# Two engines take attention a's outputs out of PSUM: in whole tiles, or in halves of the columns

## The chip, the cores and the metric

The kernel runs on one core of a Trainium2 chip. Its engines are TensorE (PE in the profile; PEld is its loading of weights), VectorE (DVE), ScalarE (ACT), GpSimd (POOL) and SyncE (SP), which here only issues DMAs. Each engine works through its own instructions in order; across engines they meet only through semaphores. The metric is the device time of one execution in microseconds, from the median of several runs.

## The reference

Sixteen sequences of 512 tokens and 256 features go through four sublayers, each added to its input after a layer norm: attention a, a gated feed-forward network, attention b, and the same network again. Attention a, cut to what matters here:

```python
q, k, v = proj(Wq, bq), proj(Wk, bk), proj(Wv, bv)          # 16 heads of 16 features
scores = jnp.einsum('bhsd,bhtd->bhst', q, k) * SCALE
scores = jnp.where(mask, scores, -jnp.inf)                  # |i - j| <= 32, or i < 4, or j < 4
attn = jax.nn.softmax(scores, axis=-1)
out = jnp.einsum('bhst,bhtd->bhsd', attn, v)                # then out @ Wo.T + bo
```

## The kernel before

The sixteen sequences are pipelined. A table (`AT`) gives each step of a sequence a place, a sequence starts 425 places after the one before, and `STEPS` is the list of all steps sorted by place. Every engine walks through this one list and issues its own part, so the order on each engine is written out by hand; there is no planner at run time. Some 132 us of the trace are one such turn, and in it steps of three or four sequences stand between each other: while attention a of one sequence is in its outputs, attention b and the feed-forward networks of earlier ones run.

Scores, probabilities' denominators and outputs share a ring of five PSUM banks (`s_bank`, 128 partitions by 512 columns of float32). `ring_places` fixes which step takes which bank; before a step writes, `pair_free` on TensorE waits until the bank's last owner has been read out, for every bank that the step takes, and only then go its matmuls.

Attention a's output of one group of four heads is the step `AV` (`a_values`, lines 919, 926 and 933: matmuls on a 64-row half of the array each). It takes two banks: one for the upper and one for the lower half of the key rows. The two have to be added. This is done in two steps:

- `AH` on ScalarE (`a_take_half`, line 1178): copies the second bank, 128x512 float32, into the SBUF tile `o_raw` (two buffers in turn), and raises `a_half`;
- `AT` on VectorE (`take_out`, line 1359): waits for `a_half`, adds the first bank to `o_raw` in place, and raises `o_taken`.

`AO` on SyncE (`store_output`, line 633) waits for `o_taken` and writes `o_raw` to DRAM. The next step of TensorE that needs the two banks waits for `a_half` (second bank) and for `o_taken` (first bank); mostly it is a pair of attention b's numerator scores, `b_pair`, line 967, which ScalarE exponentiates at line 1155 (`probs_B`). There are four groups in a sequence, so 64 takes in all: in a turn they start, in this profile's order, at places 545, 602, 627 and 648 (called first to fourth take below). Attention b's outputs need one bank and one copy (line 1365) and are not touched.

Other lines that the steps below speak of: 946 and 1165 are attention b's denominator scores and their exponentials with a sum (each followed by a short read of the accumulator), 1148 are attention a's exponentials, 1183 and 1431 split transposed inputs, 1218 writes the rotated queries and keys, 1412 to 1422 are the layer norm's last steps on VectorE, 1496 and 1498 take attention values out in pieces of 256 columns, 574 and 711 are DMA issues of SyncE (packed queries and keys, the next input).

Of the kernel before, what the change touches and what calls it, by code (L numbers as in the profile page):

```python
# [8 lines left out]
ACT = mybir.ActivationFunctionType  # L9
AX = mybir.AxisListType  # L10

SEQS, S, D = 16, 512, 256
# [4 lines left out]
GROUPS = 4  # L17
# [289 lines left out]
def build(nc, x_in, Wq, bq, Wk, bk, Wv, bv, Wo, bo, Wqkv, Wout, bout, w_gate, w_up, w_down,  # L307
# [7 lines left out]
    with ctx:  # L315
        def sb(name, shape, dt):
            return ctx.enter_context(nc.sbuf_tensor(name, shape, dt))

        def sem(name):
            return ctx.enter_context(nc.semaphore(name))  # L320
# [68 lines left out]
        o_raw = [sb(f"o_raw{i}", [P, S], F32) for i in range(2)]  # L389
# [46 lines left out]
        a_half = sem("a_half")  # L436
# [11 lines left out]
        o_taken = sem("o_taken")  # L448
# [63 lines left out]
        def score_bank(kind, n, q, e=0):  # L512
            return s_bank[RINGS[kind, n, q][e][0]]
# [213 lines left out]
        def _(pe):  # L727
# [15 lines left out]
            for n, bank in enumerate(banks):  # L743
# [4 lines left out]
                if n >= len(all_banks):  # L748
                    last = n - len(all_banks)
                    pe.wait_ge(w_taken if last < NSPLIT else w_staged, last + 1 if last < NSPLIT else last - NSPLIT + 1)  # L750
                for c0, a in bank:
                    last = pe.transpose(all_banks[n % len(all_banks)][:, c0:c0 + P], a, eye[:, :])
# [10 lines left out]
            def pair_free(kind, n, q):  # L763

                for _, before in RINGS[kind, n, q]:
                    if before is None:
                        continue
                    kind, n, r, e = before
                    if kind == "A1":
                        pe.wait_ge(a1_taken, r * UNITS["A"] + 2 * n + e + 1)  # L770
                    elif kind == "TM":
                        pe.wait_ge(ntopT_ready, r + 1)
                    elif kind == "A2":
                        pe.wait_ge(a_exp, r * UNITS["A"] + 2 * n + e + 1)
                    elif kind == "AV" and e:
                        pe.wait_ge(a_half, r * GROUPS + n + 1)
                    elif kind == "AV":
                        pe.wait_ge(o_taken, TAKE["A", n, r] + 1)
                    elif kind == "DP":
                        pe.wait_ge(den_exp, r * UNITS["D"] + 2 * n + e + 1)  # L780
                    elif kind == "DT":
                        pe.wait_ge(rden_ready["B"], r + 1)
                    elif kind == "BV":
                        pe.wait_ge(o_taken, TAKE["B", n, r] + 1)
                    else:
                        pe.wait_ge(b_exp, r * UNITS["N"] + 2 * n + e + 1)
# [92 lines left out]
            def a_pair(kind, p, q):  # L879
                pair_free(kind, p, q)  # L880
                if p == 0 and kind == "A1":
                    pe.wait_ge(blocks_ready, q + 1)
                    a_far_first(q)
                elif p == 0:
                    pe.wait_ge(ntopT_ready, q + 1)
                    a_far_second(q)
                else:
                    if kind == "A1" and p == 1 and q == 0:
                        pe.wait_ge(c_in, 16 * NC)
                        pe.wait_ge(fills_in, 48)  # L890
                    if kind == "A1" and p % 2:
                        pe.wait_ge(a_packed[p // 2], (q + 1) * 96)
                    elif p == 1:
                        pe.wait_ge(ntop_in, (q + 1) * 128)
                    a_near(kind, p, q)

            def turn_maxima(q):
                pair_free("TM", 0, q)
                pe.wait_ge(ntop_ready, q + 1)
                bank = score_bank("TM", 0, q)[0:2 * HEADS, :]  # L900
                pe.matmul(bank[:, 0:GLOBALS], ntop[:, NT, :], glob_sel[:, :], start=True, stop=True, skip_group_check=True)
                for t in range(NT):
                    a = GLOBALS if t == 0 else 0
                    last = pe.matmul(bank[:, t * P + a:(t + 1) * P], ntop[:, t, :], eye_bf[:, a:], start=True, stop=True,
                                     skip_group_check=True)
                last.then_inc(ntop_turned, 1)

            def a_values(j, q):

                v = v_aug["A"]  # L910
                bank = [score_bank("AV", j, q, half) for half in range(2)]
                pair_free("AV", j, q)
                if j == 0:
                    pe.wait_ge(v_glob_in, (q + 1) * 16)
                    pe.wait_ge(gu_taken, gu_use("V", 1, "VA", q) + 1)
                pe.wait_ge(a_exp, q * UNITS["A"] + 2 + 4 * (j + 1))
                for t in range(NT):
                    for c in range(4):
                        pe.matmul(bank[t % 2][32 * c:32 * c + DH + 1, 0:GLOBALS], v[:, t, head(j, c), :],
                                  probs_gq[:, t, head(j, c), :], start=t < 2, stop=t >= 2,  # L920
                                  tile_position=(0, 32 * c), skip_group_check=True)

                for c in range(4):
                    for half, columns in enumerate((slice(S // 2, S), slice(GLOBALS, S // 2))):
                        r = slice(HB * half, HB * half + HB)
                        pe.matmul(bank[half][32 * c:32 * c + DH + 1, columns], v_glob[r, head(j, c), :], probs_gk[r, columns],
                                  start=False, stop=False, tile_position=(HB * half, 32 * c), skip_group_check=True)
                for t in range(NT):
                    for c in range(4):
                        for half in range(2):  # L930
                            r = slice(HB * half, HB * half + HB)
                            col, a, b = window(t, half)
                            last = pe.matmul(bank[half][32 * c:32 * c + DH + 1, a:b], v[r, t, head(j, c), :],
                                             probs["A"][r, (4 * j + c) % RING["A"], col:col + b - a], start=False, stop=True,
                                             tile_position=(HB * half, 32 * c), skip_group_check=True)
                last.then_inc(a_used, 1)
# [196 lines left out]
        def _(act):  # L1133
# [38 lines left out]
            def a_take_half(j, q):  # L1172

                take = TAKE["A", j, q]
                if take // 2:
                    act.wait_ge(o_out[take % 2], take // 2 * 16)
                act.wait_ge(a_used, q * GROUPS + j + 1)
                act.activation(o_raw[take % 2][:, :], score_bank("AV", j, q, 1)[:, :], ACT.Copy).then_inc(a_half, 1)

            def x_high(block, q):  # L1180
                for k in range(KT):
# [38 lines left out]
            for n in range(NSPLIT, NBANKS):  # L1220
                act.wait_ge(w_turned, n + 1)
                bank, m = all_banks[n % len(all_banks)], n - NSPLIT
                if m < 8:
                    dst, k, half = (st_gT, st_uT)[m // 4], m // 2 % 2, m % 2
# [5 lines left out]
            for _, kind, n, block, q in STEPS:  # L1230
                if kind == "A2E":
                    a_exponential(2 * n, q)
                    a_exponential(2 * n + 1, q)
                elif kind == "TC":
                    keep_maxima(q)
                elif kind == "AH":
                    a_take_half(n, q)
                elif kind == "DE":
                    den_exponential(2 * n, q)
                    den_exponential(2 * n + 1, q)  # L1240
                elif kind == "NE":
                    b_exponential(2 * n, q)
                    b_exponential(2 * n + 1, q)
                elif kind == "XH":
                    x_high(block, q)
                elif kind == "GT":
                    half_tanh(block, n, q)
                elif kind == "T1":
                    qk_step(block, n, q)
                elif kind == "W2":  # L1250
                    rot_high_step(n, q)
# [3 lines left out]
        def _(dve):  # L1255
# [29 lines left out]
            for t in range(KT):  # L1285
                for c2 in range(2):
# [3 lines left out]
                    last = dve.tensor_copy(dst, a)  # L1290
# [63 lines left out]
            def take_out(kind, j, q):  # L1354

                take = TAKE[kind, j, q]
                if kind == "A":
                    dve.wait_ge(a_half, q * GROUPS + j + 1)
                    dve.tensor_tensor(o_raw[take % 2][:, :], o_raw[take % 2][:, :], score_bank("AV", j, q)[:, :], ALU.add)\  # L1359
                        .then_inc(o_taken, 1)  # L1360
                    return
                if take // 2:
                    dve.wait_ge(o_out[take % 2], take // 2 * 16)
                dve.wait_ge(b_used, q * GROUPS + j + 1)
                dve.tensor_copy(o_raw[take % 2][:, :], score_bank("BV", j, q)[:, :]).then_inc(o_taken, 1)
# [317 lines left out]
```

## Time and profile before

| | us |
|---|---|
| median of 3 runs | 2285.48 (2284.11 to 2287.06) |
| the profiled execution's own time | 2279.23 |
| its span, first to last instruction | 2277.5 |
| TensorE busy | 1931.6 (85%) |
| ScalarE busy | 1445.5 (63%) |
| VectorE busy | 1387.9 (61%) |

The span is that of one execution under the profiler; 1.7 us of its own time lie around it. Busy times are those of the whole span, and each stretch of a turn has another limit, so the chain of work that ended last is what tells where a microsecond counts. The mean granted clock of TensorE is 0.936 of full speed.

### The profile page before, as it was taken

How to read it: one execution, taken by the hardware profiler on the slowest of the kernel's cores; microseconds unless marked ns; L12 is line 12 of the kernel's file. 1: busy time of each engine (PE TensorE's matmuls, PEld its weight loads, DVE VectorE, ACT ScalarE, POOL GpSimd, SP SyncE). 2: the span in 40 equal slices, each digit the busy share in tenths (PEclk: the TensorE clock that was granted, in tenths of full speed). 3: DMA queues.
4: the chain of work that ended last, by engine and by line, in shares of the span. 5: the costliest groups of instructions: out<-in, count | busy, mean ns of one | idle time of the engine just before them, and what ended most of it. 6: DMA issues, size and time to landing. Idle time of an engine off the chain costs nothing.

```text
span 2277.5 us, 63345 instructions
## 1 busy us (share of the span) xinstructions
PE 1931.6 (85%) x25221; PEld 1387.7 (61%) x25221; DVE 1387.9 (61%) x2971; ACT 1445.5 (63%) x3580; POOL 781.6 (34%) x1131
## 2 busy tenths in 40 slices
PE   5677879889898989989798998979898898989785
PEld 4463657666675756657576665757566675756444
DVE  5363657576575757657575765757576675755534
ACT  1227666676767667676766767676676767667580
POOL 0023233334323333332333343233334334334331
PEclk8798999999999999999999999999999999999887
DMA  7214344252434424243442524343342434333221
GB/s 186 71 42 95 60 114 92 76 111 72 105 67 121 85 78 109 69 105 68 118 88 78 108 71 106 66 122 84 82 106 74 110 73 109 83 90 85 70 63 34
DMA packets 129636, 201.87 MB, mean 89 GB/s; under 512 B 26768, under 2 KB 60560, under 8 KB 129312
## 3 DMA queue, kind: packets, MB, share of 16 engines
q1 hardware_dynamic: 129344, 197.80, 36.2%
q8 instruction: 205, 3.36, 0.6%
q14 instruction: 87, 0.71, 0.1%
HBM read 67.87 MB, written 51.52 MB: 52 GB/s over the span
## 4 chain that ended last, share of the span: by engine, by line
PE 57%; ACT 16%; DVE 11%; SPq 6%; DMA 5%; issue 4%; POOL 1%; POOLq 0%; ACTq 0%; DVEq 0%
PE gu_bank L1051 15%; PE d_bank L1067 7%; ACT s_bank L1165 6%; PE gu_bank L1079 6%; SPq L574 5%; PE s_bank L982 5%; PE s_bank L946 4%; ACT probs_B L1155 4%; PE gu_bank L1015 3%; PE gu_bank L1002 3%; PE s_bank L812 2%; PE s_bank L967 2%; DMA pack_b<-src_b 2%; PE gu_bank L1025 2%; PE s_bank L820 2%
## 5 line engine op out<-in xcount | busy, mean ns | idle before, releaser
L1165 ACT ACTIVATE s_bank<-s_bank 128x512 f32<-128x512 f32 x1024 | 602.5, 591 | 171.9 <-PE s_bank L946 171.3
L1574 POOL TENSOR_TENSOR h<-tmp,h 128x512 fp32r<-128x512 f32 x192 | 252.0, 1313 | 448.0 <-DVE h L1455 448.0
L1155 ACT ACTIVATE probs_B<-s_bank 128x512 f32<-128x512 f32 x640 | 334.5, 611 | 47.4 <-PE s_bank L967 44.8
L1051 PE MATMUL gu_bank<-xT,w_g 128*128 128x256 f32 x1536 | 231.5, 294 | 28.2 <-DVE tmp L1438 23.1
L946 PE MATMUL s_bank<-pack_b 48*128 48x512 f16 x1024 | 182.7, 400 | 82.4 <-DMA pack_b<-src_b 69.4
L1051 PE MATMUL gu_bank<-xT,w_u 128*128 128x256 f32 x1536 | 239.2, 296 | 3.2 <-DVE tmp L1444 0.5
L1051 PEld LDWEIGHTS gu_bank<-xT,w_g 128*128 128x128 f32 x1536 | 205.0, 196 | 55.2 <-DVE tmp L1438 37.6
L1194 ACT ACTIVATE tmp<-gu_bank 128x512 f32<-128x512 f32 x192 | 114.6, 597 | 192.7 <-PE gu_bank L1051 184.5
L1067 PE MATMUL d_bank<-w_d,h 128*128 128x256 f32 x1536 | 225.5, 289 | 3.3 <-POOL h L1574 3.3
L1051 PEld LDWEIGHTS gu_bank<-xT,w_u 128*128 128x128 f32 x1536 | 205.5, 196 | 36.6 <-issue 20.4
L1438 DVE SCALAR_TENSOR_TENSOR tmp<-tmp,gu_bank 128x512 f32<-128x512 f32 x192 | 130.8, 682 | 148.3 <-ACT tmp L1194 146.8
L1591 POOL TENSOR_SCALAR_AFFINE_SELECT probs_B<-probs_B 128x256 f32<-128x256 f32 x512 | 193.1, 412 | 42.7 <-ACT probs_B L1155 42.6
L1067 PEld LDWEIGHTS d_bank<-w_d,h 128*128 128x128 f32 x1536 | 196.8, 189 | 17.1 <-issue 7.9
L1165 ACT ACTIVATION_READ_ACCUMULATOR s_bank<-s_bank 128x1 f32 x1024 | 196.2, 192 | 0.0
L1444 DVE TENSOR_TENSOR tmp<-tmp,gu_bank 128x512 f32<-128x512 f32 x192 | 132.0, 688 | 83.9 <-PE gu_bank L1051 82.0
L1557 POOL TENSOR_TENSOR veps<-mv,eps 128x4 f32<-128x4 f32 x64 | 12.9, 202 | 489.6 <-DVE mv L1408 489.6
L967 PE MATMUL s_bank<-pack_b 48*128 48x512 f16 (+3 forms) x1024 | 116.7, 310 | 72.9 <-DVE o_raw L1359 32.4
L1328 DVE TENSOR_REDUCE top<-s_bank 128x4 f32<-128x512 f32 x256 | 161.0, 684 | 5.0 <-PE s_bank L820 5.0
L1148 ACT ACTIVATE probs_A<-s_bank 128x512 f32<-128x512 f32 x256 | 133.5, 602 | 46.2 <-PE s_bank L820 45.3
L982 PE MATMUL s_bank<-probs_B,v_aug_B 128*16 128x512 f32 (+3 forms) x2048 | 156.2, 447 | 2.6 <-POOL probs_B L1591 2.3
L812 PE MATMUL s_bank<-band,eye_bf 64*64 64x512 bf16 x1024 | 110.4, 419 | 27.7 <-DMA pack_a<-src_a 14.0
L946 PEld LDWEIGHTS s_bank<-pack_b 48*128 48x128 f16 x1024 | 41.4, 94 | 145.7 <-DMA pack_b<-src_b 72.1
(140 smaller groups left out, 3320.6 us busy)
## 6 DMA issues: line engine op xcount, KB each, us to landing
pack_b<-src_b SPq DMA_DIRECT2D x768, 64.0 KB, 2.5
pack_a<-src_a SPq DMA_DIRECT2D x384, 64.0 KB, 2.3
x<-in_L_attn_a_x_dram SPq DMA_DIRECT2D x32, 512.0 KB, 4.9
o_scr_A<-o_raw SPq DMA_DIRECT2D x64, 256.0 KB, 2.4
o_scr_B<-o_raw SPq DMA_DIRECT2D x64, 256.0 KB, 2.1
xn<-o_scr_A SPq DMA_DIRECT2D x32, 256.0 KB
rden_on<-r_scr_A SPq DMA_DIRECT2D x32, 256.0 KB
x_scr<-x SPq DMA_DIRECT2D x16, 512.0 KB, 2.9
```

The lines of the kernel that those rows point to most:

```text
L812: pe.matmul(bank[e][HB * half:HB * half + HB, :], eye_of(e), rows_of(band, e, half), start=True, stop=False, tile_position=(HB * e, HB * h ...
L946: pe.matmul(score_bank("DP", n, q, e)[:, :], pack_b[r, j % 2, 0, 0, tile, t * P:(t + 1) * P], pack_b[r, j % 2, 0, 1, tile, :], start=True, ...
L967: last = pe.matmul(bank[e][:, c0:c0 + S - t * P], pack_b[r, j % 2, 1, 1, tile, t * P:(t + 1) * P], pack_b[r, j % 2, 1, 0, tile, t * P:S], ...
L982: last = pe.matmul(bank[32 * c:32 * c + DH, t * P:S], v_aug["B"][:, t, head(j, c), 0:DH], probs["B"][:, n, c0:c0 + S - t * P], start=t == ...
L1051: last = pe.matmul(bank[:, f * D:(f + 1) * D], plain(w[:, k, c:c + P], exact), plain(given[:, k, half * D:(half + 1) * D], exact), start=k ...
L1067: last = pe.matmul(bank[:, t, :], plain(h[part][:, i % 2, c:c + P], exact), plain(w_d[:, 2 * pair + f, :], exact), start=pair == 0 and f = ...
L1079: last = pe.matmul(bank[:, :], w_part[:, k, n * P:(n + 1) * P], given[part][:, k, :], start=k == 0 and i == 0, stop=k == KT - 1 and i == 2)
L1155: act.activation(probs["B"][:, i, :], score_bank("NP", n // 2, q, n % 2)[:, :], ACT.Exp, scale=SM_SCALE)\
L1165: act.activation(bank[:, :], bank[:, :], ACT.Exp, scale=SM_SCALE, accum_out=den[:, 0, j, 2 * tile + e, t:t + 1]).then_inc(den_exp, 1)
L1328: dve.reduce_max(dst, a, AX.X).then_inc(a1_taken, 1)
L1574: pool.tensor_tensor(h[1][:, i % 2, :], tmp[:, i % 2, :], h[0][:, i % 2, :].bitcast(F32), ALU.subtract)\
L1591: ins = pool.affine_select(a, a, [[0, 2], [1, P]], ALU.is_ge, 0.0, base=0, channel_multiplier=-1)
```

## The change

ScalarE copies the second bank in two instructions of 256 columns each and raises `a_half` after each. VectorE adds in two instructions of 256 columns each, waiting for one more of `a_half` before each, and raises `o_taken` after the second only. TensorE's wait for the second bank counts two per take. The same elements are computed from the same operands; no step moves to another place in any engine's list.

```diff
                     elif kind == "AV" and e:
-                        pe.wait_ge(a_half, r * GROUPS + n + 1)
+                        pe.wait_ge(a_half, 2 * (r * GROUPS + n + 1))
...
                 act.wait_ge(a_used, q * GROUPS + j + 1)
-                act.activation(o_raw[take % 2][:, :], score_bank("AV", j, q, 1)[:, :], ACT.Copy).then_inc(a_half, 1)
+                for columns in (slice(0, S // 2), slice(S // 2, S)):
+                    act.activation(o_raw[take % 2][:, columns], score_bank("AV", j, q, 1)[:, columns], ACT.Copy).then_inc(a_half, 1)
...
                 if kind == "A":
-                    dve.wait_ge(a_half, q * GROUPS + j + 1)
-                    dve.tensor_tensor(o_raw[take % 2][:, :], o_raw[take % 2][:, :], score_bank("AV", j, q)[:, :], ALU.add)\
-                        .then_inc(o_taken, 1)
+                    for n, columns in enumerate((slice(0, S // 2), slice(S // 2, S))):
+                        half = o_raw[take % 2][:, columns]
+                        dve.wait_ge(a_half, 2 * (q * GROUPS + j) + n + 1)
+                        last = dve.tensor_tensor(half, half, score_bank("AV", j, q)[:, columns], ALU.add)
+                    last.then_inc(o_taken, 1)
                     return
```

## Rows read from the trace of the kernel before

**Rows 1.** The profile's page: the chain that ended last, shares by engine and line.
```profile
PE 57%; ACT 16%; DVE 11%; SPq 6%; DMA 5%; issue 4%; POOL 1%; POOLq 0%; ACTq 0%; DVEq 0%
```
**Rows 2.** The two lines of the take: instructions, idle before, who waits (us, times).
```profile
L1178 ACT ACTIVATE o_raw<-s_bank x64: 576/597/597, 78.6 to 2046.1; 128x512 f32<-128x512 f32 x64
...
L1359 DVE TENSOR_TENSOR o_raw<-o_raw,s_bank x64: 686/689/689, 79.2 to 2046.8; 128x512 f32<-128x512 f32 x64
  ACT o_raw L1178: 119.0, 63
...
  PE s_bank L967: 32.4, 27
  PE s_bank L946: 1.4, 1
```
**Rows 3.** The chain in order of time (start, length, what): a first take; first and last.
```profile
92.40 0.60 ACT o_raw L1178
...
1081.68 0.60 ACT o_raw L1178
1082.31 0.70 DVE o_raw L1359
1083.01 0.14 issue
1083.14 0.42 PE s_bank L967 x4
1083.57 1.89 ACT probs_B L1155 x4
...
2046.13 0.60 ACT o_raw L1178
```
**Rows 4.** Groups by shape, all of the span: busy, mean ns | idle before.
```profile
L1148 ACT ACTIVATE probs_gq<-s_bank 128x256 f32<-128x256 f32 x16 | 6.1, 384 | 4.2 <-PE s_bank L875 4.2
L1496 DVE TENSOR_TENSOR v_aug_A<-gu_bank,v_bias 128x256 f32<-128x256 f32 x64 | 23.9, 414 | 2.8 <-PE gu_bank L1002 2.7
```
**Rows 5.** ScalarE in order of time (start, length), around a first take.
```profile
1071.56 0.19 ACT L1165 ACTIVATION_READ_ACCUMULATOR s_bank<-s_bank 128x1 f32 x1
1071.65 0.59 ACT L1165 ACTIVATE s_bank<-s_bank 128x512 f32<-128x512 f32 x1
1081.68 0.60 ACT L1178 ACTIVATE o_raw<-s_bank 128x512 f32<-128x512 f32 x1 [0.59 <-PE s_bank L933]
1082.17 1.08 ACT L1155 ACTIVATE probs_B<-s_bank 128x512 f32<-128x512 f32 x2
1083.56 2.06 ACT L1155 ACTIVATE probs_B<-s_bank 128x512 f32<-128x512 f32 x4 [0.30 <-PE s_bank L967]
```
**Rows 6.** VectorE in order of time, the same stretch.
```profile
1082.31 0.69 DVE L1359 TENSOR_TENSOR o_raw<-o_raw,s_bank 128x512 f32<-128x512 f32 x1 [1.14 <-ACT o_raw L1178]
1082.91 0.15 DVE L1412 SCALAR_TENSOR_TENSOR newton<-root 128x4 f32<-128x4 f32 x1
1083.10 0.16 DVE L1415 TENSOR_TENSOR newton<-newton,veps 128x4 f32<-128x4 f32 x1
1083.50 1.38 DVE L1422 TENSOR_SCALAR xn<-x,mv,root 128x256 f32<-128x256 f32 x4
1086.14 1.29 DVE L1431 TENSOR_TENSOR xT<-gu_bank,xT 128x512 fp32r<-128x512 f32 x2 [0.40 <-ACT xT L1183]
```
**Rows 7.** ScalarE around a second and a third take.
```profile
1100.86 0.63 ACT L1218 ACTIVATE src_b<-tmp 128x512 f16<-128x512 f32 x1 [0.62 <-POOL tmp L1579]
...
1116.11 0.58 ACT L1178 ACTIVATE o_raw<-s_bank 128x512 f32<-128x512 f32 x1
...
1118.12 0.58 ACT L1165 ACTIVATE s_bank<-s_bank 128x512 f32<-128x512 f32 x1 [0.23 <-PE s_bank L946]
```
**Rows 8.** TensorE around a fourth take that is not in the chain.
```profile
856.66 0.61 PE L967 MATMUL s_bank<-pack_b 48*128 48x512 f16 x6 [1.25 <-DVE o_raw L1359]
```
**Rows 9.** The chain in the same turn: its longest piece, before the next statistics.
```profile
853.28 6.36 DMA x<-in_L_attn_a_x_dram
```

## The prediction

> **What bounds the kernel now.** I read the chain of work that ended last before the busy shares: no engine fills the span, so only the chain tells where a microsecond counts. By engine it is TensorE with 57%, ScalarE 16%, VectorE 11% [rows 1]: a relay of short pieces in which one engine hands over to the next. The reader should then ask of the two changed lines whether they are such a handover. They are. VectorE sits idle before 63 of its 64 adds until ScalarE's copy ends (119.0 us), and TensorE then sits idle 28 times until the add ends (32.4 + 1.4 us) [rows 2]. In order of time the chain runs copy 0.60, add 0.70, 0.14 of issue, then four matmuls of line 967 and the exponentials on them [rows 3]. I counted this pair in the chain from its start to its end: 23 of the 64 takes are in it, the first at 92.40, the last at 2046.13 [rows 3]. Fourteen of them are first takes, one in every turn from 285 us on, six are fourth takes, three lie in the start-up.
>
> The other 41 takes are not in the chain. Where a fourth take is missing from it, TensorE still idles 1.25 us for the add [rows 8], but the chain of that turn runs through the transfer of the next input, 6.36 us [rows 9]. A shorter take there brings nothing.
>
> **The length of one take.** Before: the add starts 1082.31 - 1081.68 = 0.63 us after the copy and lasts 0.69, so the end comes 1.32 us after the copy's start [rows 5, 6].
>
> After, from the nearest shapes. ScalarE takes 256 columns of PSUM to SBUF in 0.384 us (line 1148), VectorE's tensor_tensor with 256 columns lasts 0.414 us (line 1496) [rows 4]. Halving the columns thus takes away only about a third of the time: 0.597 to 0.384, 0.689 to 0.414; the two halves together record 0.77 and 0.83. But a record overlaps the next one of its engine. ScalarE starts its next instruction 0.49 us after one of 0.60, and 0.09 us after one of 0.19 [rows 5]: 0.11 and 0.10 before the record's end, for 512 columns and for one alike. From the first half to the second that makes 0.28 us; I take 0.30, as the second is a copy with a full 256 columns to write. On VectorE four of 256 columns take 1.38 us, (1.38 - 0.41) / 3 = 0.32 apart [rows 6]; I take 0.33 for a tensor_tensor, whose record is slightly longer. The handover between the engines keeps its 0.03.
>
> - first copy 0.00 to 0.384; second copy 0.30 to 0.684
> - first add starts at 0.384 + 0.03 = 0.414
> - second add starts at the later of 0.414 + 0.33 = 0.744 (VectorE itself) and 0.684 + 0.03 = 0.714 (its wait): 0.744
> - it ends at 0.744 + 0.414 = 1.158
>
> The take ends 1.32 - 1.158 = 0.16 us sooner. It is VectorE's two adds in a row, not ScalarE, that set this end.
>
> Bounds of that step, since no row shows a second add waiting for a second copy. If neither engine overlaps its halves: copies end at 0.384 and 0.768, the first add at 0.828, and the second starts after another 0.03, the gap that lines 1412 and 1415 show where one waits for the other (0.19 apart at 0.15 each) [rows 6]; end 1.27, gain 0.05. The other end is the sum above with nothing lost, 0.17. I stay near the upper one, as the overlaps are in rows of the same kind.
>
> **What it costs the two engines.** ScalarE gets to its next instruction 2 x 0.30 = 0.60 us after the copy's start instead of 0.49: 0.11 later (0.28 later if the two halves did not overlap: 0.77 - 0.49). VectorE gets to its own 0.744 + 0.33 = 1.07 after the copy's start instead of 0.63 + 0.60 = 1.23: earlier by 0.16, since until then it only waited. What covers ScalarE's 0.11, take by take:
>
> - first take: two exponentials of line 1155 follow at once, then ScalarE is idle 0.30 until TensorE's matmuls of line 967 [rows 5], and could have started some 0.1 before the last record's end, so 0.40 of cover. TensorE comes 0.16 sooner, ScalarE 0.11 later: 0.40 - 0.16 - 0.11 = 0.13 is left, and the whole 0.16 gets through. The splitting add of line 1431 still waits 0.40 for ScalarE [rows 6] and moves along.
> - second take: 0.62 of idle before the next instruction [rows 7].
> - third take: it stands inside a closed run of line 1165, with no idle before it; four instructions later ScalarE is idle 0.23 for matmuls of line 946 [rows 7]. That covers the 0.11. With its cover gone the price would be 16 x 0.11 = 1.8 us.
> - fourth take: the same two exponentials and the same idle stretch as in the first.
>
> VectorE's 64 more instructions add 64 x (0.83 - 0.69) = 9 us and ScalarE's 64 x (0.77 - 0.60) = 11 us of recorded busy time. By the walk above they cost the path nothing, because VectorE waits before the take and ScalarE behind it.
>
> The Trainium skill speaks against such a split: "VectorE: DVE Perf Modes", section "The TRN2 errata", says that ScalarE and VectorE pay a fixed latency per instruction and advises pieces of at least 512 elements. The rows agree with the fixed part (0.384 for half of 0.597 [rows 2, 4]). The same skill's "Perfetto Trace Analysis", section "Optimizing Scalar/DVE Operations", says that where these engines are not saturated but make others idle, breaking instructions up may let work end sooner; the idle times of [rows 2] are that situation. By the first rule alone the sum would be a loss, and the last rival below is that case.
>
> The other edits: TensorE's wait for the second bank is the same instruction with another number, and the second copy ends at 0.684 instead of 0.60, yet TensorE needs both banks and the add's 1.158 stays last. SyncE's store of `o_raw` waits for the second add and so can only go 0.16 sooner. Nothing moves past any queue.
>
> **The sum.** 23 takes in the chain x 0.16 = 3.7 us. The chain behind a first take is matmuls, exponentials, splitting, all waiting for each other [rows 3, 6], so the gain is carried on and not met by an engine that was late anyway. Profiled execution: 2279.23 - 3.7 = 2275.5. The median of the runs stands 2285.48 - 2279.23 = 6.25 us above it, a gap that the change doesn't touch: **2285.48 - 3.7 = 2281.8 us**, 0.16% faster. What a measurement of this kernel can tell from no change is about 0.2%, 4.6 us, so my forecast lies just inside it.
>
> **Rivals.**
>
> - *Serial halves.* The second wait keeps the halves of an engine from overlapping, or ScalarE's own next work takes over in the chain; each take gains 0.05. For: no row shows this pattern. Against: the overlaps in [rows 5, 6]. 23 x 0.05 = 1.2: 2284.3 us.
> - *More than the chain shows.* VectorE is free 0.16 sooner after every take, and TensorE stops idling sooner in all 28 places of [rows 2]; a few chains beside the last one are as close as the missing fourth takes. If ten more takes counted and the freed VectorE gave as much again in half of the turns, 33 x 0.16 + 8 x 0.16 = 6.6: 2278.9 us. Against: the transfer in [rows 9] doesn't get faster.
> - *The change doesn't do what it says*: the adds end when they did. Then a take ends at 1.32 as before: 2285.5 us. Against: 0.744 is VectorE's own sum and has no free term.
> - *ScalarE becomes the bound behind the copies* (slower). The place is ScalarE's stretch behind the first, third and fourth take. If a copy of 256 columns held ScalarE as long as one of 512, so 0.49, it would come to its exponentials 0.49 later against a cover of 0.40, and in the third take against 0.23 + 0.10 = 0.33. Price: 23 x 0.09 + 16 x 0.16 = 4.6 us, 2290.1 us, with the gain of the takes gone as well. It decides from a delay of 0.33 on; at 0.28 it costs nothing. For: the fixed part is two thirds of a short instruction. Against: the 0.09 after a record of 0.19 [rows 5]. The errata section named above is the rule that would have it so, if its fixed cost stood between the halves; the rows show most of it inside them.
>
> **How the numbers follow.** Forecast 0.50; serial halves 0.18; more than the chain shows 0.18; no effect 0.04; ScalarE the bound 0.10. Around each stands a scatter of some 1.5 us, the half width of the three runs' spread, and a little for transfers and banks that fall into place differently. Faster by over 0.2% (below 2280.9): nearly all of the second rival and 0.35 of the forecast, 0.36. Slower by over 0.2% (above 2290.1): half of the last, whose middle lies on that bound, and 0.02 for transfers that fall worse, 0.07. Within: 0.57. The range reaches from the better rival's middle, 2277, to 2287.5, which leaves out the slower rival and the far tail of the better one.
>
> **What would show it.** In the profile after: 128 copies of about 0.384 and 128 adds of about 0.41; the second copy 0.30 after the first, the second add 0.33 after the first, the take's end 1.16 after its start; TensorE's idle time on the add down from 33.8 to about 33.8 - 28 x 0.16 = 29.3 us; ScalarE's busy time up by 11, VectorE's by 9; ScalarE still idle behind the first take and the third. Wrong would be: ScalarE without idle time before its third exponential behind a first take, halves that don't overlap, or a chain in which the takes are as many as before and a transfer has grown by what they lost.

## The result, and the profile after

The changed kernel takes 2271.99 us (median of 9 runs, 2265.46 to 2279.67), the kernel before 2282.07 us (median of 9, 2273.19 to 2287.06). The ratio is 0.9960, 95% interval 0.9944 to 0.9976: faster by 0.4%, some 9 us, where the forecast said 3.7 us and the range ended at 2277. A second measurement on another occasion (e2 below) gave 0.9963. The profiled execution took 2274.38 us, its span is 2272.7 us.

The two lines of the take after the change (number, durations, idle before, who waits), which answer to [rows 2]:

```profile
L1179 ACT ACTIVATE o_raw<-s_bank x128: 365/379/384, 80.1 to 2041.5; 128x256 f32<-128x256 f32 x128
...
L1362 DVE TENSOR_TENSOR o_raw<-o_raw,s_bank x128: 411/418/423, 80.5 to 2042.0; 128x256 f32<-128x256 f32 x128
...
  ACT o_raw L1179: 106.9, 63
...
  PE s_bank L967: 29.4, 28
```

The same first take as in [rows 3, 5, 6], first the chain, then the two engines (start, length, what):

```profile
1079.41 0.39 ACT o_raw L1179
...
1079.82 0.76 DVE o_raw L1362 x2
1080.58 0.14 issue
1080.72 0.42 PE s_bank L967 x4
1081.14 1.89 ACT probs_B L1155 x4
```
```profile
1079.41 0.66 ACT L1179 ACTIVATE o_raw<-s_bank 128x256 f32<-128x256 f32 x2 [0.59 <-PE s_bank L933]
1079.95 3.25 ACT L1155 ACTIVATE probs_B<-s_bank 128x512 f32<-128x512 f32 x6
1083.06 1.12 ACT L1184 ACTIVATE xT<-gu_bank 128x512 fp32r<-128x512 f32 x2
```
```profile
1079.82 0.75 DVE L1362 TENSOR_TENSOR o_raw<-o_raw,s_bank 128x256 f32<-128x256 f32 x2 [0.92 <-ACT o_raw L1179]
1083.72 1.29 DVE L1434 TENSOR_TENSOR xT<-gu_bank,xT 128x512 fp32r<-128x512 f32 x2 [0.41 <-ACT xT L1184]
```

The reader should see that the take itself is as the prediction had it. It ends 1080.58 - 1079.41 = 1.17 us after its start (forecast 1.16, before 1.32); the second copy starts 0.66 - 0.38 = 0.28 after the first, the second add 0.75 - 0.42 = 0.33 after the first; TensorE's idle time on the add is 29.4 us (forecast 29.3). The chain has 23 takes, as before. So what the forecast's 3.7 us are made of is there. What is missing in the forecast is in a column that it never read, TensorE's granted clock. These are the 8 us behind a first take, from the start of its add, in six turns of the kernel before; the clock is the third number from the end of a line:

```profile
549.84:557.84 8.00, 6.24 (x69) 4.13 (x69) 5.61 (x13) 4.91 (x10) 5.58 (x13) 1.00 0.50 174
...
814.84:822.84 8.00, 7.12 (x68) 5.01 (x69) 4.70 (x12) 4.59 (x9) 5.58 (x13) 0.79 0.51 172
948.51:956.51 8.00, 7.12 (x68) 5.00 (x69) 4.79 (x12) 4.59 (x9) 5.58 (x13) 0.79 0.49 171
1082.31:1090.31 8.00, 6.24 (x69) 4.13 (x69) 5.62 (x13) 4.91 (x10) 5.58 (x13) 1.00 0.47 171
1214.46:1222.46 8.00, 7.17 (x68) 4.88 (x69) 4.70 (x12) 4.58 (x9) 5.59 (x13) 0.79 0.47 170
1346.97:1354.97 8.00, 6.24 (x69) 4.13 (x69) 5.61 (x13) 4.91 (x10) 5.58 (x13) 1.00 0.51 172
```

and in three of the changed one:

```profile
815.09:823.09 8.00, 6.24 (x69) 4.13 (x69) 5.61 (x14) 5.12 (x11) 5.74 (x13) 1.00 0.50 173
947.02:955.02 8.00, 7.06 (x67) 4.87 (x68) 4.69 (x13) 4.87 (x10) 5.74 (x13) 0.79 0.50 172
1079.82:1087.82 8.00, 6.24 (x69) 4.14 (x69) 5.61 (x14) 5.12 (x11) 5.74 (x13) 1.00 0.47 168
```

A mean of 0.79 over 8 us is 3.4 us at the lower level (1.2 GHz, half of full) and the rest at the upper one (2.4 GHz): (1 - 0.79) x 8 = 1.7 us of full clock lost. The expectations below count low clock in this lost time, 1.7 us a drop, and so do I from here on. It stands in 3 of 13 turns of the kernel before and in 1 of 13 of the changed one. (The 13 turns, here and below, are the whole ones between the fourteen first takes from 285 us on.) In front of it TensorE did nothing for 1.25 us, the wait for the add; it waits as long in the turns without a drop. The matmuls in the stretch run slower: of the same turn at 948.51, and of the one at 1082.31 in full clock:

```profile
951.81 0.64 PE L812 MATMUL s_bank<-band,eye_bf 64*64 64x512 bf16 x4
952.24 0.61 PE L820 MATMUL s_bank<-pack_a 50*64 50x96 f16 x16
...
1085.31 0.41 PE L812 MATMUL s_bank<-band,eye_bf 64*64 64x512 bf16 x4
1085.55 0.38 PE L820 MATMUL s_bank<-pack_a 50*64 50x96 f16 x16
```

What one such drop costs can be read off the starts of the adds. From the first take's add (948.51 and 1082.31) to the second take's:

```profile
967.31 0.69 DVE L1359 TENSOR_TENSOR o_raw<-o_raw,s_bank 128x512 f32<-128x512 f32 x1 [1.64 <-ACT o_raw L1178]
...
1100.27 0.69 DVE L1359 TENSOR_TENSOR o_raw<-o_raw,s_bank 128x512 f32<-128x512 f32 x1 [1.64 <-ACT o_raw L1178]
```

18.80 us with a drop, 17.96 without, and the ten turns without one all lie at 17.96 or 17.97, the three with one at 18.80 to 18.89. In the changed kernel it is 17.81 to 17.83 in twelve turns and 18.73 in the one with the drop. So the halves give 0.15 us to every turn, and a drop costs 0.84 to 0.93 up to the second take. Whole turns, from one first take to the next, show that this is not won back later: with a drop they last 133.3 us on average, without one 132.2, and in the second profile of this kernel (e1) 133.3 and 131.7; other differences between turns are in these means too.

### The profile page after: what moved, and what is told of

The parts are those of the page before. It is cut to its first block, busy times and chain, and to the rows that moved or that the text cites. A ratio compares the mean times of both kernels' runs of the same rounds, so it can differ in the third digit from the quotient of the medians.

```text
span 2272.7 us, 63473 instructions
## 1 busy us (share of the span) xinstructions
PE 1932.3 (85%) x25221; PEld 1389.3 (61%) x25221; DVE 1392.9 (61%) x3035; ACT 1449.0 (64%) x3644; POOL 782.3 (34%) x1131
## 4 chain that ended last, share of the span: by engine, by line
PE 57%; ACT 16%; DVE 10%; SPq 6%; DMA 5%; issue 4%; POOL 1%; POOLq 0%; ACTq 0%; DVEq 0%
PE gu_bank L1051 15%; PE d_bank L1067 7%; ACT s_bank L1165 6%; PE gu_bank L1079 6%; SPq L574 6%; PE s_bank L982 5%; PE s_bank L946 4%; ACT probs_B L1155 4%; PE gu_bank L1002 3%; PE gu_bank L1015 3%; PE s_bank L812 2%; DMA pack_b<-src_b 2%; PE s_bank L967 2%; PE gu_bank L1025 2%; PE s_bank L820 2%
## 5 line engine op out<-in xcount | busy, mean ns | idle before, releaser
L967 PE MATMUL s_bank<-pack_b 48*128 48x512 f16 (+3 forms) x1024 | 117.6, 312 | 69.3 <-DVE o_raw L1362 29.4
```

Source lines behind the costliest of these rows:

```text
L967: last = pe.matmul(bank[e][:, c0:c0 + S - t * P], pack_b[r, j % 2, 1, 1, tile, t * P:(t + 1) * P], pack_b[r, j % 2, 1, 0, tile, t * P:S], ...
```

## The experiments

All ratios are to the kernel before, run beside each kernel on the same chip, with 95% intervals. "Drops" are the turns out of 13 whose 8 us behind the first take hold a stretch at the lower level; the next column is the time from the first take's add to the second's in turns without a drop, from the same profile. A profile is one execution; the ratio comes from all of them.

| | ratio | interval | drops | us, no drop |
|---|---|---|---|---|
| kernel before | 1 | | 3 | 17.96 |
| e1 before, again | 1.0012 | 0.9999 to 1.0025 | 6 | 17.96 |
| changed kernel | 0.9960 | 0.9944 to 0.9976 | 1 | 17.82 |
| e2 changed, again | 0.9963 | 0.9946 to 0.9980 | 0 | 17.82 |
| e3 shorter take | 0.9941 | 0.9920 to 0.9963 | 0 | 17.63 |
| e4 longer take | 1.0053 | 1.0034 to 1.0072 | 11 | 18.30 |
| e5 first take only | 0.9968 | 0.9950 to 0.9985 | 0 | - |
| e6 the other three | 0.9981 | 0.9967 to 0.9995 | 8 | - |
| e7 kept busy | 0.9959 | 0.9946 to 0.9972 | 0 | 17.97 |
| e8 banks swapped | 0.9985 | 0.9972 to 0.9998 | 9 | 17.76 |
| e9 halves, busy | 0.9928 | 0.9906 to 0.9950 | 0 | 17.81 |
| e10 busy at two takes | 0.9911 | 0.9887 to 0.9935 | 0 | 17.81 |
| e11 busy in the transfer's wait | 0.9957 | 0.9939 to 0.9975 | 6 | 17.96 |
| e12 all together | 0.9896 | 0.9869 to 0.9924 | 0 | 17.82 |

(In e5 and e6 one take of the pair is halved and the other not, so the starts of their adds don't compare.)

**e1, the kernel before again.** No edit but a helper that gives the same counts.

> The kernel before, with whole-tile copies and adds as before (only the counting of a_half goes through a helper that gives the same numbers). Every theory: no change, ratio 1.000. Its interval tells how much of the measured 0.4% such a comparison can find by itself: if it comes out at 0.998 or 1.002, an effect of that size is not shown by five rounds.

Measured 1.0012: no effect, though the interval shows that such a comparison can be off by 0.1%. What it adds is its profile: 6 of 13 turns with a drop where the first profile had 3. The number of drops varies between executions of one kernel, and single executions vary by 10 us and more.

**e2, the changed kernel again.**

> The changed kernel again, on another occasion. Theory A (relay): 23 takes of the chain x 0.16 us = 3.7 us faster, ratio 0.9984; the 0.996 of the first measurement was partly scatter. Theory B (the relay plus more: each saved microsecond is paid back a second time, by a higher granted TensorE clock or by takes that the chain of one execution doesn't show): 9 us faster, ratio 0.996 again, with the granted clock some 0.003 higher than before.

0.9963, and a mean granted clock over its runs of 0.941 beside 0.935 for the kernel before. Theory A alone (0.9984) lies outside the interval.

**e3, a shorter take, and e4, a longer one.**

```diff
# e3: the copies, then the adds (one half of the columns only)
+                for first, end in ((S // 2, S), (0, S // 2)):
...
+                    for first, end in ((S // 2, S),):
# e4
+                    last = dve.reduce_max(spare[:, q * GROUPS + j:q * GROUPS + j + 1], score_bank("AV", j, q)[:, 0:S // 2], AX.X)
                     last.then_inc(o_taken, 1)
```

> Leaves out the addition for the first 256 columns: ScalarE copies both halves as in the change (second half of the columns first), VectorE adds one half only. The take ends 0.41 + 0.41 = 0.83 us after the copy's start in place of 1.32: 0.49 shorter, three times the change's 0.16. Theory A: 23 x 0.49 = 11 us faster than the kernel before, ratio 0.995. Theory B (2.4 times as much for each microsecond): 27 us faster, 0.988. Theory C (chance alignment of transfers, not the length of the take, made the 0.4%): nothing in proportion, anything between 0.994 and 1.000.

> The kernel before with one more VectorE instruction of 256 columns (a maximum over half of the first bank, into a spare column) between the add and o_taken: the take ends 0.33 us later and VectorE is free 0.33 us later. Theory A: 23 x 0.33 = 7.6 us slower, ratio 1.0033; more if fourth takes come into the chain that were beside it. Theory B: 18 us slower, 1.008, and a lower granted clock. Theory C: between 1.000 and 1.004 without proportion to the other dose.

e4: 1.0053, 12 us, between A's 7.6 and B's 18. Drops in 11 of 13 turns, and without one the stretch is 18.30, the 0.34 us longer that the extra instruction takes. 23 x 0.33 = 7.6 us and (11 - 5.75) / 13 x 14 x 0.87 = 4.9 us for the drops make 12.5. Here 5.75 is the mean of the four profiles with whole, uncovered first takes (before, e1, e6 and e11: 3, 6, 8, 6), 14 is the number of first takes from 285 us on, and 0.87 is near the middle of the 0.74 to 0.93 us that the 23 drops of these profiles cost. The time alone doesn't call for the clock, though: in e4's own chain stand 29 adds, not 23, as 13 fourth takes are in it, and 29 x 0.33 = 9.6 us lie inside the interval (8 to 16 us). What e4 adds is the count of the drops.

e3: 0.9941, 13 us (interval 8 to 18); B's 27 is out and A's 11 would fit. A take shorter by 0.49 gives only 17.96 - 17.63 = 0.33 to a turn: past that, ScalarE is the later one, which is what the prediction's cover for it said (0.40 less the delay of its own copies, measured 0.05). So A's own number here is 23 x 0.33 = 7.6 and not 11. And drops can't go below none: 7.6 + 5.75 / 13 x 14 x 0.87 = 7.6 + 5.4 = 13.0. Longer is slower and shorter is faster, in the order of the doses: Theory C (chance alignment of transfers) is out.

**e5 and e6, which takes.** `DVE_AT` and `ACT_AT` hold the column bounds of each take:

```diff
# e5
+ACT_AT = {0: [0, 256, 512], 1: [0, 512], 2: [0, 512], 3: [0, 512]}
+DVE_AT = {0: [0, 256, 512], 1: [0, 512], 2: [0, 512], 3: [0, 512]}
# e6
+ACT_AT = {0: [0, 512], 1: [0, 256, 512], 2: [0, 256, 512], 3: [0, 256, 512]}
+DVE_AT = {0: [0, 512], 1: [0, 256, 512], 2: [0, 256, 512], 3: [0, 256, 512]}
```

> Halves in the first take of a turn only, the other three as before. Theory A (relay alone): 14 links x 0.16 = 2.2 us faster, ratio 0.999. Theory B (relay plus clock: TensorE's idle time at the first take is what lets its granted clock fall in the 8 us behind it, in 3 to 6 of 13 turns of the kernel before, in 0 to 1 of the changed one, at 1.7 us of low clock each): 2.2 us and the clock's part, some 14 x 4.5/13 x 0.85 = 4 us, together 6 us, ratio 0.9973, and next to no turn with low clock in those 8 us.

> Halves in the second, third and fourth take only. Theory A: 9 links x 0.16 = 1.4 us faster, ratio 0.9994. Theory B: the same 1.4 us, since the low clock behind the first take stays as often as before (3 to 6 of 13 turns). If this one gains 6 us and the one with the first take alone doesn't, Theory B has the wrong place.

0.9968 against an expected 0.9973 with no drop at all, and 0.9981 against 0.9994 with 8 drops. The place is as Theory B has it: with the first take halved the profile shows no drop, with the others halved it shows 8. e6's interval reaches from 1.1 to 7.5 us and takes the 1.4 in, at its edge.

**e7, TensorE kept at work while the take stays as long.**

```diff
+                if p == 18 and RINGS["NP", 19, q][0][1] is not None and RINGS["NP", 19, q][0][1][:2] == ("AV", 0):
+                    r = RINGS["NP", 19, q][0][1][2]
+                    pe.wait_ge(a_half, r * GROUPS + 1)
+                    for _ in range(3):
+                        pe.matmul(score_bank("NP", 19, q, 0)[:, :], pack_b[0:ROWS, j % 2, 1, 1, 0, 0:P],
+                                  pack_b[0:ROWS, j % 2, 1, 0, 0, :], start=True, stop=True, tile_position=(0, 0),
+                                  skip_group_check=True)
                 pair_free("NP", p, q)
```

> Whole-tile takes as before; but while TensorE waits for the add of a first take, it runs three more 512-column matmuls (on operands already there) into the bank that ScalarE's copy has released; the scores that follow overwrite them. The take is as long as before, 1.32 us. Theory B: TensorE is idle some 0.6 us in place of 1.25, no turn with low clock in the 8 us behind the first take, some 4 us faster, ratio 0.998. Theory A: nothing gained, 1.000, or a little lost if the three matmuls end after the add.

This is the run that decides. The add of a first take, and TensorE in order of time, the three added matmuls in line 964:

```profile
1068.95 0.69 DVE L1366 TENSOR_TENSOR o_raw<-o_raw,s_bank 128x512 f32<-128x512 f32 x1 [1.14 <-ACT o_raw L1185]
...
1068.97 0.82 PE L964 MATMUL s_bank<-pack_b 48*128 48x512 f16 x3 [0.44 <-ACT o_raw L1185]
1069.78 0.61 PE L974 MATMUL s_bank<-pack_b 48*128 48x384 f16 x8
```

and the 8 us behind two first takes:

```profile
282.87:290.87 8.00, 7.06 (x72) 4.34 (x72) 5.61 (x13) 4.89 (x10) 5.35 (x12) 1.00 0.50 175
...
1068.95:1076.95 8.00, 7.06 (x72) 4.34 (x72) 5.61 (x13) 4.89 (x10) 5.58 (x13) 1.00 0.49 173
```

The scores of line 974 start 1069.78 - 1068.95 = 0.83 us after the add's start, as before (1083.14 - 1082.31 [rows 3]), and the turn's first stretch is 17.97 or 17.98 (18.21 in one turn): nothing is handed over sooner. TensorE's idle time falls from 1.25 to 0.44 us. No turn has a drop, and the kernel is 0.41% faster (interval 0.28 to 0.54%), as much as with the halves. Work that computes nothing made the kernel faster, so idle time of TensorE, not the length of the take alone, is what the rest of the gain was about. The profile is of this kernel's fastest execution, 2255.74 us where the other five took 2269 to 2273, so its count may flatter; but those five have a mean granted clock of 0.939 too, beside 0.934 for the kernel before.

The 9 us are more than 5.75 / 13 x 14 x 0.87 = 5.4; in its profile the fourth takes, which have no cover, also show fewer low stretches (3 of 13 turns, before 8 and 6). Whether that follows from the first takes or is chance is open.

**e8, the banks swapped.** The bank that the scores need first was the one released last.

```diff
-                    elif kind == "AV" and e:
+                    elif kind == "AV" and not e:
...
-                act.activation(o_raw[take % 2][:, :], score_bank("AV", j, q, 1)[:, :], ACT.Copy).then_inc(a_half, 1)
+                act.activation(o_raw[take % 2][:, :], score_bank("AV", j, q)[:, :], ACT.Copy).then_inc(a_half, 1)
# and the add reads bank 1
```

> Whole tiles, but the banks change places: ScalarE copies the first bank and VectorE adds the second. In the ring the first bank is the one that the scores behind a take need first, the second is needed one pair later; so TensorE's first wait ends with the copy at 0.60 + 0.10 in place of the add at 1.32 + 0.14. The pair after it still needs the add. Both theories: TensorE's 33 us of idle time on the add fall to a few; ScalarE, idle 0.30 behind its two exponentials, bounds the gain of a take at about 0.40: 23 x 0.40 = 9 us by the relay alone (0.996); by Theory B 4 us more for the clock (0.994). A rival: VectorE's and ScalarE's order behind the take was fitted to the old release, and the pair behind waits instead; then no more than the halves' 0.9963.

A miss on both theories' numbers, and the most useful one; the expectation's rival, that the engines' order behind the take was fitted to the old release, is nearest. TensorE at a first take:

```profile
1085.64 0.40 PE L967 MATMUL s_bank<-pack_b 48*128 48x384 f16 x4 [0.53 <-ACT o_raw L1178]
1086.27 0.39 PE L967 MATMUL s_bank<-pack_b 48*128 48x256 f16 x4 [0.24 <-DVE o_raw L1359]
...
1087.28 1.32 PE L1025 MATMUL gu_bank<-eye,xn 128*128 128x128 f32 x8 [0.36 <-DVE xn L1422]
```

The idle 1.25 us became 0.53 + 0.24 + 0.36: the last piece is the layer norm on VectorE, which stands behind the same add, so only 0.20 of the expected 0.40 reach the turn (17.76). And with the idle time spread over three waits and a part of the work done sooner, drops are not fewer: 9 of 13, though in the execution with the lowest clock of this kernel's twelve (0.926); their mean is 0.932, beside 0.934 for the kernel before. The relay's gain, 23 x 0.20 = 4.6 us, seems partly paid back: (9 - 5.75) / 13 x 14 x 0.87 = 3.0 us by that profile leaves 1.6, and 3.4 (0.5 to 6.4) were measured. The three pieces make 1.13 us, hardly more than the 1.10 us that had 1 drop in 39 turns, so the sum of the idle time doesn't decide alone. What else does, no run here parts.

**e9 and e10, halves and cover; e11, cover in the longest wait; e12, all.**

```diff
# e9 (p in (18,)), e10 and e12 (p in (18, 1)), on the changed kernel
+                before = RINGS["NP", p + 1, q][0][1] if p in (18, 1) else None
+                if before is not None and before[0] == "AV" and before[3] == 1:
+                    pe.wait_ge(a_half, 2 * (before[2] * GROUPS + before[1] + 1))
+                    for _ in range(2):
+                        pe.matmul(score_bank("NP", p + 1, q, 0)[:, :], eye_bf[:, :], band[0][:, :], start=True, stop=True,
+                                  skip_group_check=True)
# e11 (on the kernel before) and e12
+                if n == 0:
+                    pair_free("DP", n, q)
+                    for i in range(16):
+                        pe.matmul(score_bank("DP", n, q, i % 2)[:, :], eye_bf[:, :], band[0][:, :], start=True, stop=True,
+                                  skip_group_check=True)
                 if n % 8 == 0:
                     pe.wait_ge(u_packed[j], (q + 1) * 96)
-                pair_free("DP", n, q)
+                if n:
+                    pair_free("DP", n, q)
```

> The change (halves in all takes), and behind the first take of a turn two extra 512-column matmuls while TensorE waits, into the bank that ScalarE has released. It parts the two terms: against the whole-tile kernel with the same cover (ratio 0.9959 to the kernel before) only the relay of 23 x 0.16 = 3.7 us is left to gain, so 0.9943; against the plain halves (0.9963) almost nothing of low clock behind first takes is left to take away, so 0.9943 would need the fewer idle pieces at other places. If the clock behind the first take is all that kept_busy had, halves and cover together come out at 0.996 and the relay's term is not to be seen.

> As the kernel before it in this call, with the same two matmuls behind the fourth take as well, where 7 to 8 of 13 turns of the changed kernel run at low clock. By the slope found within the profiles (0.61 us of a turn's time for each us of low clock) and some 1.1 to 1.7 us of low clock a turn there, at most 0.61 x 1.4 x 14 = 12 us more; I expect a third of it, 4 us, since part of that idle time is not the take's: 0.9925.

> The kernel before with whole takes; in its longest idle stretch of a turn (TensorE waits 4.4 us for the packed queries and keys of attention b) sixteen extra 512-column matmuls run into the two banks that the next scores overwrite. There every turn of every kernel has low clock, 2.6 to 3.0 us. The clock theory: with TensorE at work that low clock goes, 0.61 x 2.7 x 15 = 25 us faster, 0.989. If the price of low clock is not causal (both come from something else, such as a late transfer), the time stays, or grows by what the matmuls overrun.

> All together: halves, two matmuls behind the first and the fourth take, sixteen in the transfer's wait. If the terms add: 0.989 for the transfer's wait and 0.9925 for the rest give 0.982; if the chip allows only so much work in a time and takes the clock back elsewhere, clearly less than that sum.

e9 came out at 0.9928 (expected 0.9943, inside), 0.0031 below e7: the relay's 3.7 us (0.0016) are compatible, but the intervals are too wide to see that term by itself, and the two were measured on different occasions. It is also 0.0035 below the plain halves of e2, whose profile has no drop left behind a first take that a cover could remove; what the cover gives beyond that is open, as in e7. e10's 0.9911 can't be told from e9.

e11: the stretch around the transfer's wait, before and with the cover:

```profile
1101.50:1105.50 4.00, 0.07 (x2) 0.07 (x2) 0.06 (x1) 0.96 (x2) 2.37 (x2) 0.88 0.50 118
1105.50:1109.50 4.00, 4.00 (x16) 2.97 (x17) 0.69 (x1) 1.81 (x5) 1.48 (x2) 0.50 0.65 143
```
```profile
1096.00:1100.00 4.00, 3.35 (x15) 1.49 (x16) 0.89 (x2) 1.60 (x3) 2.54 (x3) 1.00 0.62 135
1100.00:1104.00 4.00, 4.00 (x46) 3.06 (x46) 1.45 (x3) 2.84 (x8) 1.59 (x2) 1.00 0.67 179
```

The low clock behind the wait is gone in all 13 turns (it stood in all 13 before), so cause and place are as expected, but the kernel gained 10 us, not 25. From the second take's start to the third's a turn is 14.39 us in place of 15.41, 1.02 for 2.8 us of lost clock a turn. In the upper fence a part of it is lost while TensorE waits anyway (0.88 with 0.07 us busy). My slope of 0.61 us for each lost us, fitted over the turns of ten profiles, didn't hold for this stretch.

e12 is the fastest kernel of this study, 2258.34 us, 0.9896 (interval 0.9869 to 0.9924), with a mean granted clock of 0.957; its terms add up less than fully: 0.982 was expected from an e11 of 0.989, and with the measured 0.9957 and 0.9911 it would be 0.9868, just below the interval.

**The clock of every execution.** The counts of drops come from one execution each, but the mean granted clock is known for all of them. Over the 61 executions of the kernel before that stand beside e1 to e12, in three groups, the slower ones had the lower clock: within a group 0.92 us more for each 0.001 less (standard error 0.13). This goes together and is not by itself a cause, but as a price it gives an estimate that needs no profile. In the table the relay's term is the one worked out above, the clock's term is 0.92 us for each 0.001 by which the kernel's mean clock lies above that of the kernel before, and the last column is the measured gain.

| | clock, difference | relay + clock, us | measured, us |
|---|---|---|---|
| e2 | 0.0061 | 3.7 + 5.6 = 9.3 | 8.4 |
| e3 | 0.0067 | 7.6 + 6.2 = 13.8 | 13.4 |
| e4 | -0.0035 | -7.6 - 3.2 = -10.8 | -12.1 |
| e5 | 0.0062 | 2.2 + 5.7 = 7.9 | 7.3 |
| e6 | 0.0018 | 1.4 + 1.7 = 3.1 | 4.3 |
| e7 | 0.0064 | 5.9 | 9.3 |
| e8 | -0.0015 | 4.6 - 1.4 = 3.2 | 3.4 |
| e9 | 0.0090 | 3.7 + 8.3 = 12.0 | 16.4 |
| e10 | 0.0119 | 3.7 + 10.9 = 14.6 | 20.3 |
| e11 | 0.0121 | 11.1 | 9.8 |
| e12 | 0.0231 | 3.7 + 21.3 = 25.0 | 23.7 |

The six kernels without added matmuls (e2 to e6 and e8) come out within 1.3 us, and so do e11 and e12. With added matmuls behind the takes alone (e7, e9, e10) 3 to 6 us more were gained than both terms give. That part has no explanation here.

## Why the prediction was wrong

- *What bounds the kernel*: the relay was read rightly, and the places too, but from durations and waits alone. TensorE's granted clock stood in the page and in every stretch that can be asked for, and no sentence of the prediction used it.
- *The length of one take*: right to 0.01 us, with both overlaps and VectorE's two adds setting the end.
- *The cost to the engines*: ScalarE's next instruction 0.05 late in place of 0.11, its third exponential still waits for TensorE (1081.14 against some 1080.93 at its own pace). The busy times grew by 3.5 and 5.0 us, not 11 and 9: I added records where they overlap. It changed nothing.
- *The sum* is the step that failed: "23 takes in the chain x 0.16 = 3.7 us". Its first factor treats TensorE's speed as given. The change shortened an idle stretch from 1.25 to 1.10 us, and by that the granted clock falls behind it in 1, 0 and 0 of 13 turns (the changed kernel, e2, e5), where whole takes have 3, 6, 8 and 6. At 0.87 us a drop, and with 0.5 as the mean of the changed kernel's two profiles, that is (5.75 - 0.5) / 13 x 14 x 0.87 = 4.9 us more, and 3.7 + 4.9 = 8.6 stands beside the measured 9.1 and 8.4. e7, e5 and e6 show the mechanism and its place; the split into 3.7 and 4.9 is worked out from stretches of single profiles (the clock of all executions of e2 gives 5.6 for the second), and the intervals of the ratios don't part the two terms.
- *The rivals*: "More than the chain shows" named the nearest size (6.6 us) for a wrong reason; takes that the chain doesn't show had no part in it that a run shows. Serial halves and ScalarE as the bound are out by the 0.28, 0.33 and 1.17 above. The argument for the latter, that the fixed part is two thirds of a short instruction, was a wrong reading: 256 columns less take 0.597 - 0.384 = 0.213 us off, so 0.17 of the 0.384 are fixed, under a half.
- *The range* was built from these rivals and from the spread of three runs. Nine runs of the kernel before reach from 2273 to 2287 us, more than I allowed, and their median is 2282.07: of the 9.8 us between the forecast's 2281.8 and the measured 2271.99, 3.4 are the first three runs standing high, and 6.4 are the gain that the sum lacks.

## What to carry to other kernels

Before a shorter wait is priced, look at TensorE's granted clock in the stretch behind it: where it falls in some turns and not in others, the kernel stands on an edge, and 0.15 us of wait can be worth two and a half times as much. Shorter instructions at a handover pay when the two engines overlap; the gain ends where the next engine's own queue is the later one (0.33 of 0.49 us in e3). And where a wait can't be removed, spare matmuls into a bank that is about to be overwritten can keep the clock up; here that was worth as much as the change itself, partly for reasons that the runs leave open.

## What was not expected of the hardware

- An idle stretch of 1.25 us on TensorE was followed by 3.4 us at 1.2 GHz in 23 of 52 turns (four profiles), one of 1.10 us in 1 of 39. With 1.59 us (e4) it was 11 of 13, with 0.77 us (e3) none of 13. With three idle pieces of 0.53, 0.24 and 0.36 us (e8) it was 9 of 13. Each count but the first two is from a single execution.
- A copy of 256 columns on ScalarE lasts 0.379 us against 0.597 for 512, an add on VectorE 0.418 against 0.689; started back to back they stand 0.28 and 0.33 us apart.
